# Group convolution in two passes over half-width weights, two groups side by side

## The reference

```python
out = lax.conv_general_dilated(x, kernel, ..., feature_group_count=8) + b      # [B, 512, 32, 32]
out = out.reshape(B, 8, 64, 1024).transpose(0, 1, 3, 2).reshape(B, 512, 32, 32)
x = x + out
```

## Time and profile before

| what | value |
|---|---|
| median of 3 runs | 1801.58 us (1798.86 to 1802.18) |
| the profiled execution's own time | 1800.93 us |
| its span (first to last instruction) | 1799.0 us |
| TensorE busy | 1638.3 us (91%) |
| VectorE busy | 1405.4 us (78%) |
| ScalarE busy | 963.1 us (54%) |
| GpSimd busy | 1238.6 us (69%) |
| granted TensorE clock, mean | 0.964 |
| matmuls of the group convolution (L738) | 2304, 562.5 us |
| matmuls of the shuffle (L752) | 4096, 261.1 us |

### The profile page before, as it was taken

The page is one execution under the profiler, slowest core; times in us unless marked ns, Lnnn a source line. Parts: engine busy times, 40 slices in busy tenths (PEclk is TensorE's granted clock), DMA queues, the critical chain, the costliest instruction groups (busy, mean ns, idle before and its releaser), DMA issues.

```text
span 1799.0 us, 32197 instructions
## 1 busy us (share of the span) xinstructions
PE 1638.3 (91%) x10144; PEld 924.8 (51%) x10144; DVE 1405.4 (78%) x3450; ACT 963.1 (54%) x1475; POOL 1238.6 (69%) x1159
## 2 busy tenths in 40 slices
PE   2899999999999999999999999999989999997655
PEld 0555564555556465555646555554645555553221
DVE  4347788788878888787888978888887888786664
ACT  4674656566565555555565656646565565533212
POOL 0007777777777777777777777777767777777773
PEclk9999999999999999999999999999999999998666
DMA  7017677878787787778778787777778777777774
GB/s 225 1 55 230 190 246 246 274 244 263 210 278 234 238 269 258 242 221 273 223 257 255 250 268 240 253 210 259 239 230 276 247 254 214 233 232 228 249 217 151
DMA packets 142455, 412.96 MB, mean 230 GB/s; under 512 B 24518, under 2 KB 25030, under 8 KB 142150
## 3 DMA queue, kind: packets, MB, share of 16 engines
q0 software_dynamic: 92160, 302.06, 56.1%
q1 hardware_dynamic: 49814, 106.27, 15.7%
q10 hardware_dynamic: 304, 2.44, 0.6%
HBM read 339.37 MB, written 71.30 MB: 228 GB/s over the span
## 4 chain that ended last, share of the span: by engine, by line
PE 51%; DVE 15%; issue 12%; POOL 8%; ACT 7%; DMA 6%; ACTq 0%; DVEq 0%; POOLq 0%
PE bank L738 19%; POOL sb_rows L319 8%; PE bank L720 8%; PE bank L752 7%; DMA sb_rows<-table,sb_ridx 5%; DVE sb_rows L536 4%; PE bank L711 4%; PE bank L827 4%; DVE sb_val L544 4%; PE bank L727 3%; PE bank L770 3%; ACT sb_split L395 3%; DVE sb_split L577 3%; PE bank L805 3%; DMA sb_diff<-w_off 1%
## 5 line engine op out<-in xcount | busy, mean ns | idle before, releaser
L319 POOL DMA_INDIRECT sb_rows<-table,sb_ridx x1152 | 1236.5, 1073 | 516.2 <-issue 444.8
L536 DVE SCALAR_TENSOR_TENSOR sb_rows<-sb_rows,sb_frac 128x256 f32<-128x256 f32 x1152 | 497.8, 478 | 158.7 <-DMA sb_rows<-table,sb_ridx 153.7
L738 PE MATMUL bank<-sb_split,sb_wg 128*128 128x512 f16 x2304 | 562.5, 391 | 41.7 <-ACT sb_h_sb L421 23.3
L738 PEld LDWEIGHTS bank<-sb_split,sb_wg 128*128 128x128 f16 x2304 | 221.6, 99 | 332.6 <-issue 108.0
L544 DVE SCALAR_TENSOR_TENSOR sb_val<-sb_rows,sb_frac 128x128 f32<-128x128 f32 x1152 | 328.8, 347 | 15.3
L720 PE MATMUL bank<-sb_valT,sb_wd 128*128 128x512 f32 x576 | 322.7, 644 | 0.0
L349 ACT ACTIVATE sb_valT<-bank 128x512 f32<-128x512 f32 x288 | 170.6, 592 | 253.2 <-PE bank L711 252.9
L367 ACT ACTIVATE sb_conv_sb<-bank,sb_bias 128x512 f32<-128x512 f32 x256 | 173.5, 684 | 217.2 <-PE bank L738 178.5
L752 PE MATMUL bank<-sb_fold_sb,sb_conv_sb 128*64 128x64 f32 x4096 | 261.1, 280 | 1.7 <-ACT sb_conv_sb L367 1.6
L752 PEld LDWEIGHTS bank<-sb_fold_sb,sb_conv_sb 128*64 128x64 f32 x4096 | 243.8, 207 | 31.1 <-issue 27.9
L711 PE MATMUL bank<-sb_eye_sb,sb_val 128*128 128x128 f32 x1152 | 182.9, 283 | 69.8 <-DVE sb_val L544 51.1
(11 more groups left out here) (76 smaller groups left out, 1011.6 us busy)
## 6 DMA issues: line engine op xcount, KB each, us to landing
table<-sb_table_sb SPq DMA_DIRECT2D x144, 256.0 KB, 4.3
sb_xs<-x SPq DMA_DIRECT2D x64, 512.0 KB, 8.1
out<-sb_res SPq DMA_DIRECT2D x128, 256.0 KB, 3.9
sb_rows<-table,sb_ridx POOLq DMA_INDIRECT x1152, 4.4
sb_rows<-w_group ACTq DMA_DIRECT2D x2, 1152.0 KB, 14.1
sb_wd<-w_def SPq DMA_DIRECT2D x1, 576.0 KB
sb_w<-w_in SPq DMA_DIRECT2D x1, 256.0 KB
sb_w<-w_out SPq DMA_DIRECT2D x1, 256.0 KB
```

The lines of the kernel that those rows point to most:

```text
L319: pool.indirect_dma_start(out=rows[:, (c % RING) * PER + i, :], out_offset=None, in_=tables[u % 2], in_offset=bass.IndirectOffsetOnAxis(ap ...
L536: op = nc.vector.scalar_tensor_tensor(r[:, 0:2 * CH], r[:, 2 * CH:4 * CH], frac[:, parity, half * PER + i, k, 0:1], r[:, 0:2 * CH], ALU.mu ...
L738: op = nc.tensor.matmul(pair_ps[half][:, :], wg[:, g, k, :], plane(split1[:, g, :], ky + half * HROWS, kx, HROWS), start=k == 0, stop=k == ...
```

## The change

- `group_conv(image, n)`: n from 0 to 15 gives quad, half and part. Part 0 runs the 9 taps with the high weights, part 1 with the low weights, into the same rows of the accumulator. In both, the two groups of the quad are done side by side: 64 columns each, group e in rows 64 e to 64 e + 63 of the accumulator. That makes 18 matmuls for a part where there were 9 for a group. The 16 parts stand at the places where the 16 convolutions stood.
- `conv_to_sbuf` only copies after part 1: 8 copies for an image. `conv_sb` has two buffers, each with both groups of a quad.
- The shuffle's products have 64 rows (those of the group) instead of 128, and the identity as the moving operand; `fold_sb` and its load are gone. A `sem_inc` of TensorE's queue stands ahead of them.
- `bias_of_h` stands at the beginning of VectorE's slot 16, ahead of `add_shuffled` and the interpolation.
- `OUT_LATE` (two of the copies stood later in their slot) is gone; the bias is loaded for 4 quads x 128 rows instead of 8 groups x 64.

```diff
-        CONV_FIRST = {3: (3, 1), 4: (4, 0), 5: (4, 1), 6: (5, 0), 7: (5, 1), 8: (6, 1), 9: (7, 0),
-                      12: (0, 1), 13: (1, 1)}
-        CONV_THEN = {2: (3, 0), 7: (6, 0), 9: (7, 1), 11: (0, 0), 12: (1, 0), 16: (2, 0), 17: (2, 1)}
+        CONV_FIRST = {3: 7, 4: 8, 5: 9, 6: 10, 7: 11, 8: 13, 9: 14, 12: 1, 13: 3}
+        CONV_THEN = {2: 6, 7: 12, 9: 15, 11: 0, 12: 2, 16: 4, 17: 5}
-        OUT_LATE = (6, 9)
...
-            def conv_to_sbuf(image, g, half):
-                act.wait_ge(conv_done, count(2 * GROUPS, image, 2 * g + half + 1))
-
-                act.wait_ge(shuf_done, count(2 * QUADS, image, 2 * ((g - 3) // 2) + 2 if g >= 3 else 0))
-                nc.scalar.activation(conv_sb[:, g % 3, half * HALF:(half + 1) * HALF], pair_ps[half][:, :],
-                                     ACT.Identity, bias=bias0[:, g:g + 1]).then_inc(conv_out, 1)
+            def conv_to_sbuf(image, n):
+                q, half, part = n // 4, n // 2 % 2, n % 2
+                if part == 0:
+                    return
+                act.wait_ge(conv_done, count(2 * QUADS, image, 2 * q + half + 1))
+
+                act.wait_ge(shuf_done, count(2 * QUADS, image, 2 * q - 2))
+                nc.scalar.activation(conv_sb[:, q % 2, half * HALF:(half + 1) * HALF], pair_ps[half][:, :],
+                                     ACT.Identity, bias=bias0[:, q:q + 1]).then_inc(conv_out, 1)
...
+                    if a2 and s == SHIFT_SLOT + 1:
+                        bias_of_h()
                     if s - 1 in SHUFFLE and (a1 if s > NEXT_SHUFFLE else a2):
...
-                    if a2 and s == SHIFT_SLOT + 1:
-                        bias_of_h()
...
-            def group_conv(image, g, half):
-                pe.wait_ge(w_low, 1)
-                pe.wait_ge(low1_done, count(2 * QUADS, image, g + 1))
-                pe.wait_ge(conv_out, count(2 * GROUPS, image, 2 * g + half - 1))
-                if g == 2:
-                    pe.wait_ge(h_done, count(2, image - 1, half + 1))
+            def group_conv(image, n):
+                q, half, part = n // 4, n // 2 % 2, n % 2
+                if part == 0:
+                    pe.wait_ge(w_low, 1)
+                    pe.wait_ge(low1_done, count(2 * QUADS, image, 2 * q + 2))
+                    pe.wait_ge(conv_out, count(2 * QUADS, image, 2 * q + half - 1))
+                    if q == 1:
+                        pe.wait_ge(h_done, count(2, image - 1, half + 1))
                 for k in range(TAPS):
                     ky, kx = divmod(k, 3)
-                    op = nc.tensor.matmul(pair_ps[half][:, :], wg[:, g, k, :],
-                                          plane(split1[:, g, :], ky + half * HROWS, kx, HROWS),
-                                          start=k == 0, stop=k == TAPS - 1)
-                op.then_inc(conv_done, 1)
+                    for e in (0, 1):
+                        op = nc.tensor.matmul(pair_ps[half][64 * e:64 * e + 64, :],
+                                              wg[:, 2 * q + e, k, part * GIN:(part + 1) * GIN],
+                                              plane(split1[:, 2 * q + e, :], ky + half * HROWS, kx, HROWS),
+                                              start=part == k == 0, stop=part == 1 and k == TAPS - 1)
+                if part == 1:
+                    op.then_inc(conv_done, 1)
 
             def shuffle(image, q, half):
 
-                pe.wait_ge(conv_out, count(2 * GROUPS, image, 4 * q + 4))
+                pe.wait_ge(conv_out, count(2 * QUADS, image, 2 * q + 2))
...
+                pe.sem_inc(pe_passed, 1)
                 for jj in range(COLS // 2):
                     for e in (0, 1):
                         j = half * (COLS // 2) + jj
                         op = nc.tensor.matmul(
                             shuf_ps[half][64 * e:64 * e + 64, jj * GIN:(jj + 1) * GIN],
-                            conv_sb[:, (2 * q + e) % 3, j:j + COLS * (GIN - 1) + 1:COLS], fold_sb[:, :],
+                            conv_sb[64 * e:64 * e + 64, q % 2, j:j + COLS * (GIN - 1) + 1:COLS],
+                            eye_sb[64 * e:64 * e + 64, 64 * e:64 * e + 64],
                             start=True, stop=True)
```

More of the change, by code:

```diff
@@ L3, with build_program @@
 from contextlib import ExitStack
-def build_program(nc, x, w_group, b_group, w_in, w_off, b_off, w_def, w_out, bn, eye, fold, blocks, offset_fold,
+def build_program(nc, x, w_group, b_group, w_in, w_off, b_off, w_def, w_out, bn, eye, blocks, offset_fold,
                   grid, tables, out):
@@ L65, in build_program @@
         wg = sb("wg", [128, GROUPS, TAPS, 2 * GIN], f16)
-        conv_sb = sb("conv_sb", [128, 3, PIX], f32)
+        conv_sb = sb("conv_sb", [128, 2, PIX], f32)
         norm1 = sb("norm1", [128, PIX], f32)
@@ L130, in build_program @@
         dve_passed = sem("dve_passed")
+        pe_passed = sem("pe_passed")
         zeroed = sem("zeroed")
@@ L186, in build_program @@
         stored = [sem(f"stored{n}") for n in range(QUADS)]
-        N_CONSTS = 12
+        N_CONSTS = 11
         POOL_GROUPS = 5
@@ L266, in load_constants @@
                 sp.wait_ge(zeroed, 1)
-                for dst, src in ((blocks_sb[:, :], blocks), (bias0[0:64, :], b_group), (bn_sb[:, :, :], bn),
-                                 (fold_sb[:, :], fold), (w1[:, :], w_in), (bias_off[0:OFFS, :], b_off),
+                for dst, src in ((blocks_sb[:, :], blocks), (bias0[:, :], b_group), (bn_sb[:, :, :], bn),
+                                 (w1[:, :], w_in), (bias_off[0:OFFS, :], b_off),
                                  (bias_off[64:64 + OFFS, :], b_off), (eye_sb[:, :], eye),
@@ L442, in step @@
                     if s == 0 and a2:
-                        conv_to_sbuf(nxt, *CONV_THEN[SLOTS - 1])
+                        conv_to_sbuf(nxt, CONV_THEN[SLOTS - 1])
                     if s - 1 in CONV_THEN and (a1 if s > NEXT_CONV else a2):
-                        conv_to_sbuf(new if s > NEXT_CONV else nxt, *CONV_THEN[s - 1])
+                        conv_to_sbuf(new if s > NEXT_CONV else nxt, CONV_THEN[s - 1])
                     if a2 and s == H_SLOT:
@@ L462, in step @@
                         sum1(SUMS[s], 0)
-                    if s in CONV_FIRST and s not in OUT_LATE and (a1 if s >= NEXT_CONV else a2):
-                        conv_to_sbuf(new if s >= NEXT_CONV else nxt, *CONV_FIRST[s])
+                    if s in CONV_FIRST and (a1 if s >= NEXT_CONV else a2):
+                        conv_to_sbuf(new if s >= NEXT_CONV else nxt, CONV_FIRST[s])
                     image, _, c = chunk_at(s, 1, t, tail, b)
@@ L478, in step @@
                         high1(APPLY[s], 0)
-                    if s in OUT_LATE and a2:
-                        conv_to_sbuf(nxt, *CONV_FIRST[s])
                     if a1 and s in SUMS:
@@ L801, in in_conv @@
                         if q == 0 and a1:
-                            pe.wait_ge(conv_out, count(2 * GROUPS, new, 3 + half))
+                            pe.wait_ge(conv_out, count(2 * QUADS, new, 1 + half))
                         elif q == 0:
-                            pe.wait_ge(conv_out, count(2 * GROUPS, nxt, 2 * GROUPS - 1 + half))
+                            pe.wait_ge(conv_out, count(2 * QUADS, nxt, 2 * QUADS - 1 + half))
                         op = nc.tensor.matmul(pair_ps[half][:, :], w1_norm[:, q * CH:(q + 1) * CH],
@@ L890, in constants @@
     eye = np.eye(128, dtype=np.float32)
-    fold = np.concatenate([np.eye(64, dtype=np.float32)] * 2)
     blocks = np.kron(np.eye(8, dtype=np.float32), np.full((16, 16), 1 / 16, np.float32))
@@ L903, in constants @@
                 grid[p, i, k] = (y + k // 3 - 1, x + k % 3 - 1)
-    return eye, fold, blocks, offset_fold, grid.reshape(128, -1)
+    return eye, blocks, offset_fold, grid.reshape(128, -1)
 def kernel(x, L0_conv_W, L0_conv_b, L1_conv_conv1_w, L1_conv_conv1_b, L1_conv_bn1_g, L1_conv_bn1_b, L1_conv_bn1_m,
@@ L917, in wide @@
         return np.stack([np.asarray(v).reshape(-1, 128).T for v in vectors], axis=-1)
-    eye, fold, blocks, offset_fold, grid = constants()
+    eye, blocks, offset_fold, grid = constants()
     bn = np.concatenate([
@@ L933 @@
         "w_out": np.asarray(L1_conv_conv2_w).T,
-        "bn": bn, "eye": eye, "fold": fold, "blocks": blocks, "offset_fold": offset_fold, "grid": grid,
+        "bn": bn, "eye": eye, "blocks": blocks, "offset_fold": offset_fold, "grid": grid,
     }
```

12 lines of the change are left out of this document (5 added, 7 removed).

## The result

The changed kernel takes 1837.13 us (median of 4 runs, 1833.45 to 1838.55); the kernel before took 1800.22 us in 4 runs. The ratio is 1.0219, with a 95% interval of 1.0192 to 1.0246: slower, by 39 us by the ratio and 37 by the medians. The profiled execution took 1837.36 us with a span of 1835.5.

The account below looks back on a forecast made before the run. TensorE's work list was taken as the bound, except a stretch of about 15 us set by VectorE. Edges +51.5, copies -10, bias -4.2, clock -4 gave +33 on span 1799.0, forecast 1835 us; own range 1815 to 1858, widened to 1762 to 1860.

Parts of the forecast that it names:

- Full rate side by side: TensorE's convolution: two 64-column groups run at once, nine pairs in the array time of nine full matmuls, no change.
- Edges, +51.5 us: TensorE's convolution parts: entering and leaving half-width blocks costs +3.6 us an image in the main stretch, +51.5 us in all.
- A: TensorE's stretch of a turn from table tile to end of slot 15's shuffle: 87.1 of 102.1 us before the change.
- Shuffle unchanged: TensorE's shuffle: loads with half the rows at the same 64-byte spacing take as long, 1.98 us a shuffle.
- Rival 1: TensorE's shuffle: separate rows halve each load step, -0.91 us a shuffle, about 1750 us in all; chance 0.22.
- Rival 2: TensorE's shuffle: row tiles writing one PSUM bank take turns, +1.8 us a shuffle, about 2020 us; chance 0.05.
- Copies, -10 us: ScalarE's convolution copies: 8 of 16 an image go, and with them TensorE's waits for them, -10 us.
- Bias of h, -4.2 us: VectorE's slot 16: bias made earlier, TensorE's wait moves from h to the table tile, 0.3 us a turn, -4.2 us.
- Clock, -4 us: TensorE's half-clock stretches at slot 16, 1.1 us in about 7 of 14 turns: half the loss goes, -4 us.
- Rival 3: TensorE's convolution: edges between a part and transposes cost next to nothing, 1784 us; chance 0.05.
- rival 4: TensorE's idle time from slot 16 to table tile vanishes altogether, up to -19 and -8 us, 1808 us; chance 0.06.
- GpSimd as the next bound: GpSimd waits 59.2 us for TensorE, 4.2 us an image; TensorE may get faster by about that and no more.

Follow-up runs that it names:

- Experiment 2: Changed kernel with each part as nine full-width matmuls of 128 weight columns (not the reference's convolution): 1788.93 us, ratio 0.9949 to the kernel before.
- experiment 3: Changed kernel with shuffle products over all 128 rows again: 1843.91 us, ratio 1.0259 to the kernel before.
- experiment 4: Changed kernel with ScalarE's copy laying each shuffle product's 64 pixels side by side, so loads read neighbours: 1798.21 us, ratio 1.0003 to the kernel before.
- experiment 5: Kernel before with the same neighbouring-column copy, shuffle loads still over all 128 rows: 1802.47 us, ratio 1.0025 to the kernel before.
- experiment 1: Kernel before with only the bias of h moved to the beginning of VectorE's slot 16: 1793.57 us, ratio 0.9987 to the kernel before.
- Experiment 6: Changed kernel with VectorE's low parts of the last quad moved ahead of the add in slot 16: 1807.38 us, ratio 1.0049 to the kernel before.
- experiment 8: Kernel before with neighbouring shuffle columns, bias of h first and low parts of the last quad first: 1782.47 us, ratio 0.9921 to the kernel before.
- experiment 7: Changed kernel with the CONV_FIRST parts moved to just ahead of CONV_THEN, so some touch: 1848.55 us, ratio 1.0297 to the kernel before.

## Why the prediction was right

The forecast was 1835 us, the result is 1837.13. The mechanism, edges of half-width blocks in TensorE's list, held; that the sum came within 2 us is in part luck. For the step on copies one more wait of the kernel before is needed, from its first 212 us; the changed kernel has none there:

```profile
PE bank L738 <- ACT sb_conv_sb L367: 6.4, 3, 3.0
```

By its steps:

- *Full rate side by side*: right, twice the matmuls in the same busy time.
- *Edges, +51.5 us*: right in each part (ahead 0.09, exit 0.13 for 0.11, behind 0.05 and 0.10 for 0.11). With the measured pieces A should be 9 x 0.27 + 3 x 0.32 + 2 x 0.23 = 3.85 us longer; it lost 7 x 0.07 in the shuffles and the copy wait of slot 12, 5.6 / 12 = 0.47: +2.9, and 90.11 - 87.1 = 3.0 was found. Experiment 2 gives 49 us for all edges, and experiment 3 shows an exit go where the tile shape stays the same.
- *Shuffle unchanged*: right but for 0.06 us or so (rows, by experiment 3). The reason given, spacing and not rows, is shown by experiments 4 and 5. Rival 1 is refuted by the result (200 ns a load against 207) and by the same two: with all 128 rows a load falls as much. The rule of the Trainium skill that stood behind it ("TensorE: Matmul & The Clock Gate", Part 3, on row groups) gave nothing here: with 64-row loads in different rows a shuffle takes 1.91 us for 1.97, and with neighbouring columns 1.08 us in both forms. Rival 2's price is refuted too: 1.91 us where it had 3.8. But the price was too high. A product of 64 moving columns takes about 0.107 us of the array (an estimate, 64/512 of the 0.86 us of L720's pair), so 16 of them in turn would need 1.72 us, which fits in 1.91. What shows that row tiles don't take turns is experiment 4, where the 16 products into one bank take 1.08 us. For these products the Trainium skill's Gotcha 1 of "TensorEngine Tiling (Array Packing)" therefore doesn't hold.
- *Copies, -10 us*: near in the waits. The 5.6 us in the middle went, and so did the 6.4 us of the start-up shown above. No run prices them alone. What the change gives without edges is 9 us by experiment 2, for copies, shuffle, bias and clock together, where the prediction had 18.
- *Bias of h, -4.2 us*: right in kind and near in size. The wait moved to the table tile (1.71 us a turn against 1.5 forecast; 2.1 on average, since other turns wait for gathers too), and experiment 1 measures 2 us by the ratio, within an interval that reaches from 6 faster to 1 slower, and 5.7 by the medians.
- *Clock, -4 us*: this step failed. The idle time moved behind the offset convolution, and the clock fell there as often (7 stretches), at 1.7 to 2.5 us a time instead of 1.1: some 5 us more lost in this profile where 4 less was forecast. "Half of the loss gone" had no row behind it.
- *Rivals 3 and 4*: the edges are there in every turn (3), and the idle time moved instead of going (4). Experiment 6 shows what rival 4 is worth where it is made true: 31 us.
- *GpSimd as the next bound*: not the first one met, though nothing of the forecast but rival 1 hung on it. Experiment 4 shortened TensorE's list and met ScalarE and VectorE before it; only in experiment 8 do GpSimd and its gathers weigh more than TensorE. A wait by the engine thought next (59.2 us) tells how far that engine is away, not that no other is nearer.

So 9 us of the gains did not come, most of it the clock, and the edges were 2 us too dear. That should make +40 where the forecast had +33; measured are +39 by the ratio, +37 by the medians and +36.5 by the spans of the two profiles. In these two profiles the thirteen steady turns grew by more than forecast, from 103.2 to 106.6 us each, 44 in all, and the stretches outside them gave 7 back: 5.6 of it in the start-up, where the kernel before had those waits and 7 us at half clock that the changed one has not. That this offset the dearer turns is the lucky part.

## What to carry to other kernels

Half-width matmuls in pairs run at full rate, but each block of them costs about 0.27 us at its two edges; count the edges, not the columns. Fewer and longer stretches of such blocks save edges (0.13 us where two parts touched in experiment 7), as long as no copy loses its cover by it. Ahead of moving a step that an engine waits for, sum that engine's and the supplier's work over the stretch: if the supplier has no pause, the wait only moves. Then look for work of the supplier that fits in its idle time ahead of the stretch; here that gave 31 us where moving the bias gave 2 to 6.

## What the runs showed of the hardware

- A float32 weight load of 64 columns takes 200 ns from every 16th float and 135 ns from neighbours, whether 64 or 128 rows are read (200 against 207, 135 against 138).
- ScalarE's write of 512 columns to places 64 floats apart takes 1153 ns instead of 685. Here the price of the spaced layout moved from the reader (a shuffle 0.83 us shorter) to the writer (a copy 0.47 us longer).
- The fall to 1.2 GHz came behind about half of the waits at the table tile (7 of 14) in the changed kernel. In experiment 6 eight waits there, 6.6 us in all and 1.9 at most, brought none, and in experiment 1 one of 14 did (the longest, 3.6 us), though most were 1.9 us. What decides between two waits of equal length stays open.
- Two 64 x 64 tiles in different rows and columns that write to one bank don't take turns: 16 float32 products of 64 columns take 1.08 us (experiment 4), where one after the other would need about 1.72 (the estimate above).
